# Lane numbers and a triangle of ones kept in PSUM in two edge stages of a graph network kernel; the bias of a third by one product per group

## Chip, cores and metric

The kernel runs on one core of a Trainium2 chip. The metric is its device time in microseconds. The time of the kernel before is 13060.72 us, the median of three runs (13050.09 to 13107.98).

## What is computed

Four graph layers run over 6250 nodes with 128 channels and 206,250 directed edges (100,000 pairs in both directions and 6250 loops), sorted by receiving node `dst`. Each layer normalises `x`, applies relu, and adds its result to `x`. Cut to the parts that the change touches:

```python
# layer 1: runs over src; ew = 0 where src == dst
aggr_out = segment_sum(ew[:, None] * h[dst], src, num_nodes)
deg      = segment_sum(ew, src, num_nodes)
# layer 2: radial weights of an edge from its length, then messages
h = silu(emb @ mlp_w0 + mlp_b0)
h = silu(h @ mlp_w1 + mlp_b1)
w = (h @ mlp_w2 + mlp_b2).reshape(-1, 4, 32)
msg = segment_sum(messages(w, x[src], edge_vec), dst, num_nodes)
# layer 3: a convolution with degrees
agg = segment_sum(h[src] * norm[:, None], dst, num_nodes)
```

## The kernel before

Every layer is a node stage (dense, over all nodes) and an edge stage. An edge stage walks over tiles of 128 edges. Four tiles (U = 4) make a group, and 403 groups (EDGE_GROUPS) make a stage; buffers come in rings of R = 4 groups, and each engine's loop body holds four groups. Each engine runs its own stream of instructions, and semaphores set the order between them. There is no planner: the order of the work is written out by hand. The edge stages are called first to fourth here; the code numbers them 0 to 3.

Because the edges are sorted by `dst`, a tile's receivers lie in a window of 128 nodes that begins at the tile's first `dst` (D0, read into registers by `windows`). A sum over receivers is a product of the gathered rows with a one-hot matrix. The one-hots compare a row of lane numbers 0 to 127 with each edge's number relative to the window (REL). The row of lane numbers, `lane`, and the triangle `K[:, CT:CP]`, which is 1 where the column is smaller than the partition, are columns of the constant tile K in SBUF. `one_hots` (L179 to L184) makes the one-hots of a group in one VectorE tensor_tensor.

**Second edge stage (L833 to L1022).** It sums over `src`, which isn't sorted, so it adds into tables in DRAM by indirect DMA. Per group, VectorE makes `same` (L923: which edges of a tile share a source), four `hotW` (L925: one-hots times weight), `hotB` and `hotA` (L929, L931: low and high part of the receiver's number, for the degrees of the fourth layer), and `before` (L935: `same` times the triangle). The maximum of `before` tells which edge of a source is the last of its tile (L936 to L939), and with it VectorE writes the index of each edge's target row (L942). In every fourth group it also clips the edge lengths (L915, L916) and multiplies the radial basis (L919). TensorE makes psX (L992), psD (L995) and psV (L1001); ScalarE copies psX to `mix` (L975) and psV to `sumrows` (L979). GpSimd (POOL) then issues four scatters with addition, one for each tile (L1015), each to a table of its own. A scatter waits until the one of the same tile of the group before has landed. VectorE's index and ScalarE's `sumrows` are double buffered: they wait until the scatters of two groups back have landed (L940 and L977).

**Third edge stage (L1075 to L1278).** SyncE loads the group's source numbers and its radial basis (L1125, L1126), POOL gathers four tiles of rows (L1139), and VectorE makes the one-hots (L1208, through `one_hots`), the messages `mid` (L1214 to L1230) and adds the window sums (L1200). TensorE's step for group n waits for `hot` and `mid` of n and then interleaves two things: the radial net of group n + 2 (`radial`, L1246) and the window sums of group n (`sums`, L1260). In order: the first layer of the net (L1249), the sums of tiles 0 and 1 (four matmuls, eight instructions, since each fp32 product is two), the second layer (L1252) when ScalarE has made h1 (L1154), the sums of tiles 2 and 3, and the radial weights into psW when ScalarE has made h2 (L1156). For each of the four tiles that is an fp32 product of h2 with w2 (L1256) and a bf16 product that adds the bias (L1257): `three` has ones in three rows, and `b2row` holds the bias cut into three bf16 parts in these rows.

**Fourth edge stage (L1361 to L1427).** SyncE loads source numbers (L1377) when VectorE has finished a group four back. POOL gathers (L1389), TensorE multiplies rows with one-hots (L1425), and VectorE makes the one-hots of the next group (L1409) and then adds four windows (L1412).

Of the kernel before, what the change touches and what calls it, by code (L numbers as in the profile page):

```python
# [6 lines left out]
ALU = mybir.AluOpType  # L7
# [3 lines left out]
P = 128  # L11
# [6 lines left out]
TN = (N + P - 1) // P  # L18
NPAD = (TN + 1) * P
TG = 7  # L20
U = 4
# [89 lines left out]
def build(nc, a, out):  # L111
# [19 lines left out]
    with ctx:  # L131
# [44 lines left out]
        def nodes(table, width):  # L176
            return table[0:TN * P, :].rearrange("(t p) c -> p t c", p=P)[:, :, 0:width]

        def one_hots(dst, n):  # L179

            return nc.vector.tensor_tensor(  # L181
                dst, lane.unsqueeze(1).to_broadcast([P, dst.shape[1], P]),
                REL[:, bass.ds(n * dst.shape[1], dst.shape[1])].unsqueeze(2).to_broadcast([P, dst.shape[1], P]),
                ALU.is_equal)  # L184

# [646 lines left out]
        with ExitStack() as st:  # L832
# [20 lines left out]
            psX = ps("psX1", [P, 2, U, P])  # L853
            psV = ps("psV1", [P, 2, U, 2 * P])
            psD = ps("psD1", [P, 512])
            radius = sb("radius1", [RB, 2 * P])
            cutoff = sb("cutoff1", [RB, 2 * P])
            rounds = EDGE_GROUPS // R
# [7 lines left out]
            with nc.Block() as block:  # L866
# [31 lines left out]
                @block.vector  # L898
                def _(dve):
                    link = Chain(dve, s_chain)  # L900
                    nc.vector.memset(psD[:, 0:TN], 0.0)
                    dve.wait_ge(s_in, 32)
                    link(nc.vector.tensor_scalar(part_i[:, :], dst_i[:, :], P - 1, None, ALU.bitwise_and))
                    link(nc.vector.tensor_copy(low_f[:, :], part_i[:, :]))
                    link(nc.vector.tensor_scalar(part_i[:, :], dst_i[:, :], 7, None, ALU.logical_shift_right))
                    link(nc.vector.tensor_copy(high_f[:, :], part_i[:, :]))
                    link(nc.vector.tensor_copy(other[:, :], dst_i[:, :]))
                    link(nc.vector.tensor_tensor(other[:, :], SRC[:, :], other[:, :], ALU.not_equal))
                    link(nc.vector.tensor_tensor(weight[:, :], weight[:, :], other[:, :], ALU.mult))

                    def step(n, g, r):
                        s = r % 2
                        if r == 0:
                            dve.wait_ge(s_len, 128 * g + 128)
                            nc.vector.tensor_scalar(cutoff[:, :], radius[:, :], 1.0, float(NB ** 0.5), ALU.is_le, ALU.mult)  # L915
                            nc.vector.tensor_scalar(radius[:, :], radius[:, :], 0.0, 1.0, ALU.max, ALU.min).then_inc(s_clip, 1)  # L916
                        if r == 2:
                            dve.wait_ge(s_exp, g + 1)
                            nc.vector.tensor_tensor(radius[:, :], radius[:, :], cutoff[:, :], ALU.mult).then_inc(s_basis, 1)  # L919
                        dve.wait_ge(s_srow[r], 16 * g + 16)  # L920
                        wait_over(dve, s_mix, n - 1)
                        tile_src = SRC[:, bass.ds(n * U, U)]
                        nc.vector.tensor_tensor(same[:, s, :, :], srow[:, r, :, :], tile_src.unsqueeze(2).to_broadcast([P, U, P]), ALU.is_equal).then_inc(s_same, 1)  # L923
                        for u in range(U):
                            last = nc.vector.tensor_scalar(hotW[:, s, u, :], lane, REL[:, bass.ds(n * U + u, 1)],  # L925
                                                           weight[:, bass.ds(n * U + u, 1)], ALU.is_equal, ALU.mult)
                        last.then_inc(s_hot, 1)
                        at = bass.ds(n * U, U)
                        nc.vector.tensor_tensor(hotB[:, s, :, :], lane.unsqueeze(1).to_broadcast([P, U, P]),  # L929
                                                low_f[:, at].unsqueeze(2).to_broadcast([P, U, P]), ALU.is_equal)  # L930
                        nc.vector.tensor_tensor(hotA[:, s, :, :], lane[:, 0:TN].unsqueeze(1).to_broadcast([P, U, TN]),  # L931
                                                high_f[:, at].unsqueeze(2).to_broadcast([P, U, TN]), ALU.is_equal).then_inc(s_node, 1)
                        dve.wait_ge(s_same, n + 1)

                        link(nc.vector.tensor_tensor(before[:, :, :], same[:, s, :, :], K[:, CT:CP].unsqueeze(1).to_broadcast([P, U, P]), ALU.mult))  # L935
                        link(nc.vector.reduce_max(later[:, :], before[:, :, :], axis=AX))  # L936
                        link(nc.vector.tensor_scalar(place[:, :], tile_src, -1.0, K[:, CP:CP + 1], ALU.mult, ALU.add))
                        link(nc.vector.tensor_tensor(place[:, :], place[:, :], later[:, :], ALU.mult))
                        link(nc.vector.tensor_tensor(place[:, :], place[:, :], tile_src, ALU.add))  # L939
                        for u in range(U):  # L940
                            wait_over(dve, s_added[u], 16 * n - 16)
                        nc.vector.tensor_copy(index[:, s, :], place[:, :]).then_inc(s_index, 1)  # L942
                        dve.wait_ge(s_index, n + 1)

                    links = 5
                    link.loop(0, R * links)
                    for r in range(R):
                        step(r, 0, r)
                    link.end(1)
                    with dve.Fori(1, EDGE_GROUPS // R) as g:  # L950
                        link.loop(g - 1, R * links)
                        for r in range(R):
                            step(R * g + r, g, r)
                    link.end(EDGE_GROUPS // R - 1)
                    for n in range(EDGE_GROUPS // R * R, EDGE_GROUPS):
                        step(n, n // R, n % R)
                    dve.wait_ge(s_mix, EDGE_GROUPS)
                    nc.vector.tensor_scalar(DINV[:, :], psD[:, 0:TN], 1.0, None, ALU.add).then_inc(s_root, 1)
                    dve.wait_ge(s_root, 2)
                    link(nc.vector.reciprocal(DINV[:, :], DINV[:, :]))  # L960
# [114 lines left out]
        with ExitStack() as st:  # L1075
# [33 lines left out]
            with nc.Block() as block:  # L1109
# [135 lines left out]
                def _(pe):  # L1245
                    def radial(n, g, r, between=(lambda: None, lambda: None)):  # L1246

                        pe.wait_ge(s_base[r], 16 * g + 16)
                        nc.tensor.matmul(psA[:, 0, :], w0[:, :], base[:, r, :], start=True, stop=True).then_inc(s_h0, 1)  # L1249
                        between[0]()  # L1250
                        pe.wait_ge(s_h1, n + 1)
                        nc.tensor.matmul(psA[:, 1, :], w1[:, :], h1[:, :], start=True, stop=True).then_inc(s_h1p, 1)  # L1252
                        between[1]()
                        pe.wait_ge(s_h2, n + 1)
                        for u in range(U):
                            nc.tensor.matmul(psW[:, r % 2, u, :], h2[:, r % 2, (u % 2) * P:(u % 2 + 1) * P], w2[:, u // 2, :], start=True, stop=False)  # L1256
                            done = nc.tensor.matmul(psW[:, r % 2, u, :], three[:, :], b2row[:, :], start=False, stop=True)  # L1257
                        done.then_inc(s_w, 1)

                    def sums(n, r, tiles):  # L1260
# [100 lines left out]
        with ExitStack() as st:  # L1361
# [4 lines left out]
            rows = sb("rows3", [P, R, U, C])  # L1366
            hot = sb("hot3", [P, 2, U, P])
            psS = ps("psS3", [P, 4, 512])
            s_chain, s_hot, s_sum, s_free, s_done = (sem(n + "_e3") for n in ("s_chain", "s_hot", "s_sum", "s_free", "s_done"))
            s_rows = gathered3  # L1370
            s_index = sem("s_index_e3", R)
            with nc.Block() as block:
# [24 lines left out]
                @block.vector  # L1397
                def _(dve):
                    link = Chain(dve, s_chain)
                    link(nc.vector.memset(ACC[:, 0, :], 0.0))  # L1400
                    dve.sem_inc(s_done, R)
                    dve.sem_inc(s_free, 4)
                    one_hots(hot[:, 0, :, :], 0).then_inc(s_hot, 1)

                    def add(n, g, r):
                        if not (isinstance(n, int) and n == last):
                            one_hots(hot[:, (r + 1) % 2, :, :], n + 1).then_inc(s_hot, 1)
                        firsts = windows(dve, n * U)
                        for u in range(U):  # L1409
                            dve.wait_ge(s_sum, n * U + (u + 1))  # L1410
                            own = ACC[:, 0, bass.ds(firsts[u], P)]
                            nc.vector.tensor_tensor(own, own, psS[:, u, 0:P], ALU.add).then_inc(s_free, 1)  # L1412
                            dve.wait_ge(s_free, n * U + (u + 5))
                        dve.sem_inc(s_done, 1)
# [128 lines left out]
```

## Time and profile before

| | |
|---|---|
| median of three runs | 13060.72 us |
| the profiled execution | 13058.8 us |
| its span, first to last instruction | 13057.0 us |
| POOL busy | 7574.9 us (58%) |
| VectorE (DVE) busy | 6520.0 us (50%) |
| TensorE (PE) busy | 6219.0 us (48%) |
| mean granted TensorE clock | 0.585 |

The profile shows one execution. Times in it are microseconds from the span's start, unless marked ns. PE is TensorE's matmul and PEld its weight load, DVE is VectorE, ACT ScalarE, POOL GpSimd, SP SyncE. L12 is line 12 of the kernel. `out<-in` names the tiles that an instruction writes and reads. The granted clock is a share of 2.4 GHz. A releaser is what ended an engine's idle time by the semaphores' events; "issue" means that the profile shows nothing that the engine waited for. Lengths in the POOL rows are those of issuing an indirect DMA, not of its transfer.

### The profile page before, as it was taken

To read this page: it belongs to the slowest core of one execution; us is meant where nothing else is said; L and a number is where in the kernel's file an instruction comes from. 1 tells how busy PE (TensorE), PEld (TensorE's weight loads), DVE (VectorE), ACT (ScalarE), POOL (GpSimd) and SP (SyncE) were. 2 spreads that over 40 slices of the span, in tenths; PEclk is the share of its full clock that TensorE was granted. 3 is DMA by queue.
4 is the path that set the end of the run, shared out by engine and by line. 5 is a ranking of instruction groups with operands and counts; after the bars stand their busy time and mean duration, and the time that the engine had idled before them with its cause. 6 is when DMAs were issued, how large, how long until landed. Compare 5 with 4: busy or idle time off the path is not lost. (4 is left out here: it accounts for less than half of the span.)

```text
span 13057.0 us, 156203 instructions
## 1 busy us (share of the span) xinstructions
PE 6219.0 (48%) x30616; PEld 5225.2 (40%) x30616; DVE 6520.0 (50%) x17016; ACT 1617.6 (12%) x2488; POOL 7574.9 (58%) x6452
## 2 busy tenths in 40 slices
PE   1333333333335555555554477777777533333332
PEld 1222222222234444444443366666666423333332
DVE  3444444444445556555555566666666522232224
ACT  0111111111111111111111011111111100000000
POOL 2544445444228888888886255555555266666663
PEclk7555555555555555555555687787888755555555
DMA  3323223223536666666666111111111111111111
GB/s 89 75 75 75 74 75 75 75 75 75 92 52 96 102 98 104 100 103 100 100 99 118 36 40 38 38 39 39 40 39 40 28 43 43 43 43 44 43 42 46
DMA packets 1206936, 865.00 MB, mean 66 GB/s; under 512 B 523976, under 2 KB 1040463, under 8 KB 1206294
## 3 DMA queue, kind: packets, MB, share of 16 engines
q0 software_dynamic: 386880, 430.42, 19.4%
q1 hardware_dynamic: 818812, 430.82, 14.1%
q10 hardware_dynamic: 1036, 1.96, 0.1%
q14 instruction: 195, 1.60, 0.0%
q8 instruction: 13, 0.21, 0.0%
HBM read 712.60 MB, written 149.81 MB: 66 GB/s over the span
## 5 line engine op out<-in xcount | busy, mean ns | idle before, releaser
L1015 POOL DMA_INDIRECT sums<-sumrows,index x1612 | 2809.7, 1743 | 858.4 <-ACT sumrows L979 385.1
L529 POOL DMA_INDIRECT rows<-table,index x1612 | 1621.7, 1006 | 1833.1 <-DMA index<-in_src_batches 1351.8
L1139 POOL DMA_INDIRECT rows<-table,index x1612 | 1573.9, 976 | 1557.6 <-DMA index<-in_src_groups 1028.6
L1389 POOL DMA_INDIRECT rows<-table,index x1612 | 1569.4, 974 | 1100.4 <-DMA index<-in_src_groups 622.6
L1425 PE MATMUL psS<-hot,rows 128*128 128x128 f32 x3224 | 957.0, 463 | 1549.1 <-DMA rows<-table,index 564.3
L1425 PEld LDWEIGHTS psS<-hot,rows 128*128 128x128 f32 x3224 | 769.1, 319 | 1737.0 <-issue 927.1
L992 PE MATMUL psX<-same,hotW 128*128 128x128 f32 x3224 | 833.3, 440 | 1273.8 <-DVE hotW L925 1076.6
L992 PEld LDWEIGHTS psX<-same,hotW 128*128 128x128 f32 x3224 | 715.8, 327 | 1391.4 <-DVE hotW L925 1180.5
L667 DVE TENSOR_TENSOR ACC<-ACC,psA 128x128 f32 x1612 | 462.5, 287 | 1603.6 <-remote 754.5
L1412 DVE TENSOR_TENSOR ACC<-ACC,psS 128x128 f32 x1612 | 465.8, 289 | 1391.4 <-issue 838.9
L1264 PEld LDWEIGHTS psS<-hot,mid 128*128 128x128 f32 x6448 | 1020.3, 233 | 206.1 <-issue 143.2
L1264 PE MATMUL psS<-hot,mid 128*128 128x128 f32 x6448 | 1098.8, 325 | 2.3 <-DVE mid L1230 2.3
L1200 DVE TENSOR_TENSOR ACC<-ACC,psS 128x256 f32 x1612 | 672.2, 417 | 769.0 <-PE psS L1264 416.0
L1001 PE MATMUL psV<-win,mix 128*128 128x129 f32 x3224 | 819.9, 433 | 346.6 <-ACT mix L975 308.3
L1001 PEld LDWEIGHTS psV<-win,mix 128*128 128x128 f32 x3224 | 703.4, 321 | 398.2 <-issue 398.2
L1256 PE MATMUL psW<-w,h 128*128 128x128 f32 x3224 | 684.4, 339 | 245.5 <-issue 131.1
L181 DVE TENSOR_TENSOR hot<-K,REL 128x512 f32<-128x512 f32 x806 | 556.0, 690 | 378.1 <-issue 198.4
L1256 PEld LDWEIGHTS psW<-w,h 128*128 128x128 f32 x3224 | 580.0, 225 | 304.9 <-issue 144.7
L942 DVE CAST index<-place 128x4 int32<-128x4 f32 x403 | 82.8, 206 | 1186.7 <-DMA sums<-sumrows,index 1179.2
L735 PE MATMUL psA<-HN,rows 128*128 128x128 f32 x1624 | 458.9, 442 | 122.6 <-DVE ACC L667 111.0
L735 PE MATMUL psA<-ACC,rows 128*128 128x128 f32 x1600 | 454.4, 444 | 105.8 <-DVE ACC L667 95.4
L1252 PE MATMUL psA<-h,w 128*128 128x256 f32 x806 | 333.6, 504 | 317.5 <-issue 178.2
(266 smaller groups left out, 9601.4 us busy)
## 6 DMA issues: line engine op xcount, KB each, us to landing
win<-table SPq DMA_DIRECT2D x1612, 64.5 KB
srow<-src_f SPq DMA_DIRECT2D x403, 256.0 KB
rows<-table,index POOLq DMA_INDIRECT x4836
HN<-rel_f SPq DMA_DIRECT2D x102, 512.0 KB
relB<-rel_f SPq DMA_DIRECT2D x102, 512.0 KB
er<-limbs SPq DMA_DIRECT2D x1632, 3.0 KB
sums<-sumrows,index POOLq DMA_INDIRECT x1612
ACC<-edge_marks SPq DMA_DIRECT2D x204, 96.0 KB
```

The source lines that it names most:

```text
L181: return nc.vector.tensor_tensor(dst, lane.unsqueeze(1).to_broadcast([P, dst.shape[1], P]), REL[:, bass.ds(n * dst.shape[1], dst.shape[1]) ...
L529: nc.gpsimd.indirect_dma_start(out=rows[:, r, k, :], out_offset=None, in_=table0[:, :], in_offset=bass.IndirectOffsetOnAxis(ap=index[:, r, ...
L735: nc.tensor.matmul(psA[:, k % 4, 0:P], rows[:, r, k, 0:C], hots[s][:, k, :], start=True, stop=True).then_inc(s_sum, 1)
L992: last = nc.tensor.matmul(psX[:, s, u, :], hotW[:, s, u, :], same[:, s, u, :], start=True, stop=True)
L1001: last = nc.tensor.matmul(psV[:, s, u, 0:W1], mix[:, s, u, :], win[:, r, u, :], start=True, stop=True)
L1015: nc.gpsimd.indirect_dma_start(out=sums1[u][:, :], in_=sums[:, s, u, :], in_offset=None, compute_op=ALU.add, out_offset=bass.IndirectOffse ...
L1139: nc.gpsimd.indirect_dma_start(out=rows[:, r, u, :], out_offset=None, in_=table2[:, :], in_offset=bass.IndirectOffsetOnAxis(ap=index[:, r, ...
L1200: nc.vector.tensor_tensor(own, own, psS[:, u, :, 0:P], ALU.add).then_inc(s_free, 1)
L1256: nc.tensor.matmul(psW[:, r % 2, u, :], h2[:, r % 2, (u % 2) * P:(u % 2 + 1) * P], w2[:, u // 2, :], start=True, stop=False)
L1264: done = nc.tensor.matmul(psS[:, u, b, 0:P], mid[:, r % 2, u, b * C:(b + 1) * C], hot[:, r % 2, u, :], start=True, stop=True)
L1389: nc.gpsimd.indirect_dma_start(out=rows[:, r, u, :], out_offset=None, in_=table3[:, :], in_offset=bass.IndirectOffsetOnAxis(ap=index[:, r, ...
L1425: nc.tensor.matmul(psS[:, u, 0:P], rows[:, r, u, :], hot[:, r % 2, u, :], start=True, stop=True).then_inc(s_sum, 1)
```

## The change

In the second edge stage a new PSUM tile psK1 takes a copy of the lane numbers (`numbers`) and of the triangle (`below`), written once by VectorE ahead of the loop. hotB, hotA and `before` read these in place of `lane` and `K[:, CT:CP]`; hotW keeps `lane`. In the fourth edge stage a PSUM tile psK3 takes the lane numbers, and `one_hots` reads them there through its new argument. `one_hots` in the first and third stages keeps `lane`. In the third stage the four bias products of a group become one, over all four tiles' columns of psW, with `b2row` repeated four times as the moving operand. It is issued behind the first layer's product and starts the accumulation; the fp32 products then add to it.

```diff
--- before.py
+++ after.py
@@ -176,10 +176,10 @@
         def nodes(table, width):
             return table[0:TN * P, :].rearrange("(t p) c -> p t c", p=P)[:, :, 0:width]
 
-        def one_hots(dst, n):
+        def one_hots(dst, n, numbers=lane):
 
             return nc.vector.tensor_tensor(
-                dst, lane.unsqueeze(1).to_broadcast([P, dst.shape[1], P]),
+                dst, numbers.unsqueeze(1).to_broadcast([P, dst.shape[1], P]),
                 REL[:, bass.ds(n * dst.shape[1], dst.shape[1])].unsqueeze(2).to_broadcast([P, dst.shape[1], P]),
                 ALU.is_equal)
 
@@ -853,6 +853,8 @@
             psX = ps("psX1", [P, 2, U, P])
             psV = ps("psV1", [P, 2, U, 2 * P])
             psD = ps("psD1", [P, 512])
+            psK = ps("psK1", [P, 4, P])
+            numbers, below = psK[:, 0, :], psK[:, 1, :]
             radius = sb("radius1", [RB, 2 * P])
             cutoff = sb("cutoff1", [RB, 2 * P])
             rounds = EDGE_GROUPS // R
@@ -899,6 +901,8 @@
                 def _(dve):
                     link = Chain(dve, s_chain)
                     nc.vector.memset(psD[:, 0:TN], 0.0)
+                    nc.vector.tensor_copy(numbers, lane)
+                    link(nc.vector.tensor_copy(below, K[:, CT:CP]))
                     dve.wait_ge(s_in, 32)
                     link(nc.vector.tensor_scalar(part_i[:, :], dst_i[:, :], P - 1, None, ALU.bitwise_and))
                     link(nc.vector.tensor_copy(low_f[:, :], part_i[:, :]))
@@ -926,13 +930,13 @@
                                                            weight[:, bass.ds(n * U + u, 1)], ALU.is_equal, ALU.mult)
                         last.then_inc(s_hot, 1)
                         at = bass.ds(n * U, U)
-                        nc.vector.tensor_tensor(hotB[:, s, :, :], lane.unsqueeze(1).to_broadcast([P, U, P]),
+                        nc.vector.tensor_tensor(hotB[:, s, :, :], numbers.unsqueeze(1).to_broadcast([P, U, P]),
                                                 low_f[:, at].unsqueeze(2).to_broadcast([P, U, P]), ALU.is_equal)
-                        nc.vector.tensor_tensor(hotA[:, s, :, :], lane[:, 0:TN].unsqueeze(1).to_broadcast([P, U, TN]),
+                        nc.vector.tensor_tensor(hotA[:, s, :, :], numbers[:, 0:TN].unsqueeze(1).to_broadcast([P, U, TN]),
                                                 high_f[:, at].unsqueeze(2).to_broadcast([P, U, TN]), ALU.is_equal).then_inc(s_node, 1)
                         dve.wait_ge(s_same, n + 1)
 
-                        link(nc.vector.tensor_tensor(before[:, :, :], same[:, s, :, :], K[:, CT:CP].unsqueeze(1).to_broadcast([P, U, P]), ALU.mult))
+                        link(nc.vector.tensor_tensor(before[:, :, :], same[:, s, :, :], below.unsqueeze(1).to_broadcast([P, U, P]), ALU.mult))
                         link(nc.vector.reduce_max(later[:, :], before[:, :, :], axis=AX))
                         link(nc.vector.tensor_scalar(place[:, :], tile_src, -1.0, K[:, CP:CP + 1], ALU.mult, ALU.add))
                         link(nc.vector.tensor_tensor(place[:, :], place[:, :], later[:, :], ALU.mult))
@@ -1247,14 +1251,14 @@
 
                         pe.wait_ge(s_base[r], 16 * g + 16)
                         nc.tensor.matmul(psA[:, 0, :], w0[:, :], base[:, r, :], start=True, stop=True).then_inc(s_h0, 1)
+                        nc.tensor.matmul(psW[:, r % 2, :, :], three[:, :], b2row[:, :].unsqueeze(1).to_broadcast([P, U, P]), start=True, stop=False)
                         between[0]()
                         pe.wait_ge(s_h1, n + 1)
                         nc.tensor.matmul(psA[:, 1, :], w1[:, :], h1[:, :], start=True, stop=True).then_inc(s_h1p, 1)
                         between[1]()
                         pe.wait_ge(s_h2, n + 1)
                         for u in range(U):
-                            nc.tensor.matmul(psW[:, r % 2, u, :], h2[:, r % 2, (u % 2) * P:(u % 2 + 1) * P], w2[:, u // 2, :], start=True, stop=False)
-                            done = nc.tensor.matmul(psW[:, r % 2, u, :], three[:, :], b2row[:, :], start=False, stop=True)
+                            done = nc.tensor.matmul(psW[:, r % 2, u, :], h2[:, r % 2, (u % 2) * P:(u % 2 + 1) * P], w2[:, u // 2, :], start=False, stop=u == U - 1)
                         done.then_inc(s_w, 1)
 
                     def sums(n, r, tiles):
@@ -1366,6 +1370,7 @@
             rows = sb("rows3", [P, R, U, C])
             hot = sb("hot3", [P, 2, U, P])
             psS = ps("psS3", [P, 4, 512])
+            numbers = ps("psK3", [P, 512])[:, 0:P]
             s_chain, s_hot, s_sum, s_free, s_done = (sem(n + "_e3") for n in ("s_chain", "s_hot", "s_sum", "s_free", "s_done"))
             s_rows = gathered3
             s_index = sem("s_index_e3", R)
@@ -1397,14 +1402,15 @@
                 @block.vector
                 def _(dve):
                     link = Chain(dve, s_chain)
+                    nc.vector.tensor_copy(numbers, lane)
                     link(nc.vector.memset(ACC[:, 0, :], 0.0))
                     dve.sem_inc(s_done, R)
                     dve.sem_inc(s_free, 4)
-                    one_hots(hot[:, 0, :, :], 0).then_inc(s_hot, 1)
+                    one_hots(hot[:, 0, :, :], 0, numbers).then_inc(s_hot, 1)
 
                     def add(n, g, r):
                         if not (isinstance(n, int) and n == last):
-                            one_hots(hot[:, (r + 1) % 2, :, :], n + 1).then_inc(s_hot, 1)
+                            one_hots(hot[:, (r + 1) % 2, :, :], n + 1, numbers).then_inc(s_hot, 1)
                         firsts = windows(dve, n * U)
                         for u in range(U):
                             dve.wait_ge(s_sum, n * U + (u + 1))
```

## Rows read from the trace of the kernel before

**Rows 1.** Windows: the second, third and fourth edge stage, with column names.

```profile
core 0: us, PE busy (x) PEld busy (x) DVE busy (x) ACT busy (x) POOL busy (x), PEclk, DMA share, GB/s
3820.00:7125.00 3305.00, 1713.45 (x8036) 1519.68 (x8034) 1952.30 (x5522) 565.53 (x1006) 2809.74 (x1612) 0.51 0.66 100
7366.00:10275.00 2909.00, 2264.86 (x12896) 1880.89 (x12896) 1847.44 (x5238) 508.73 (x905) 1573.88 (x1612) 0.81 0.16 39
10448.00:12933.00 2485.00, 956.99 (x3224) 769.12 (x3224) 737.48 (x2011) 0.00 (x0) 1569.44 (x1612) 0.50 0.17 43
```

**Rows 2.** Groups by line, second stage: busy us, mean ns, idle before it, releasers.

```profile
L1015 POOL DMA_INDIRECT sums<-sumrows,index x1612 | 2809.7, 1743 | 858.4 <-ACT sumrows L979 385.1 <-issue 349.9 <-DMA sums<-sumrows,index 121.2
...
L942 DVE CAST index<-place 128x4 int32<-128x4 f32 x402 | 82.7, 206 | 1186.6 <-DMA sums<-sumrows,index 1179.2 <-issue 3.9 <-DVE place L939 3.3
```

**Rows 3.** Line L1015 by itself: minimum, median and maximum in ns.

```profile
L1015 POOL DMA_INDIRECT sums<-sumrows,index x1612: 1541/1542/3251, 3820.5 to 7121.8; - x180
```

**Rows 4.** Timeline, second stage: start, length, line, [idle before it, releaser].

```profile
3820.52 1.61 POOL L1015 DMA_INDIRECT sums<-sumrows,index  x1 [365.29 <-ACT sumrows L979]
...
5003.68 0.68 DVE L935 TENSOR_TENSOR before<-same,K 128x512 f32<-128x512 f32 x1
5003.87 1.90 POOL L1015 DMA_INDIRECT sums<-sumrows,index  x1 [0.30 <-issue]
...
5015.31 3.20 POOL L1015 DMA_INDIRECT sums<-sumrows,index  x1 [0.30 <-DMA sums<-sumrows,index]
5015.54 0.68 DVE L929 TENSOR_TENSOR hotB<-K,low_f 128x512 bf16<-128x512 f32 x1
...
5016.42 0.68 DVE L935 TENSOR_TENSOR before<-same,K 128x512 f32<-128x512 f32 x1
...
7103.62 3.13 POOL L1015 DMA_INDIRECT sums<-sumrows,index  x1 [0.30 <-DMA sums<-sumrows,index]
```

**Rows 5.** Timeline, fourth stage, VectorE and POOL.

```profile
11501.28 0.69 DVE L181 TENSOR_TENSOR hot<-K,REL 128x512 f32<-128x512 f32 x1 [2.54 <-issue]
...
11512.28 0.69 DVE L181 TENSOR_TENSOR hot<-K,REL 128x512 f32<-128x512 f32 x1 [0.26 <-DVE ACC L1412]
...
11515.67 0.29 DVE L1412 TENSOR_TENSOR ACC<-ACC,psS 128x128 f32 x1
11515.80 0.94 POOL L1389 DMA_INDIRECT rows<-table,index  x1 [0.30 <-issue]
...
11518.15 0.69 DVE L181 TENSOR_TENSOR hot<-K,REL 128x512 f32<-128x512 f32 x1 [0.67 <-DVE ACC L1412]
11518.30 1.35 POOL L1389 DMA_INDIRECT rows<-table,index  x1 [0.30 <-issue]
```

**Rows 6.** Groups by line, fourth stage (first row) and third stage.

```profile
L1389 POOL DMA_INDIRECT rows<-table,index x1612 | 1569.4, 974 | 1100.4 <-DMA index<-in_src_groups 622.6 <-issue 477.7
...
L1200 DVE TENSOR_TENSOR ACC<-ACC,psS 128x256 f32 x1612 | 672.2, 417 | 769.0 <-PE psS L1264 416.0 <-DMA K<-in_consts 322.1 <-issue 25.2
...
L1214 DVE TENSOR_TENSOR dot<-rows,HN 128x384 f32<-128x384 f32 x403 | 222.6, 552 | 10.8 <-DMA rows<-table,index 8.2 <-issue 2.6
...
L1226 DVE TENSOR_TENSOR mid<-psW,rows 128x384 f32<-128x384 f32 x403 | 221.8, 550 | 0.0
...
L1252 PE MATMUL psA<-h,w 128*128 128x256 f32 x806 | 333.6, 504 | 317.5 <-issue 178.2 <-ACT h L1154 139.0
L1249 PE MATMUL psA<-base,w 16*128 16x256 f32 x806 | 329.0, 492 | 138.2 <-DMA base<-basis 61.6 <-DVE mid L1230 51.1 <-issue 17.1
```

**Rows 7.** Windows: the stretch of the third stage shown next.

```profile
9011.00:9021.00 10.00, 8.14 (x60) 6.66 (x58) 7.14 (x20) 1.42 (x3) 6.89 (x7) 1.00 0.19 50
```

**Rows 8.** Timeline, TensorE, third stage, granted clock 1.00.

```profile
9011.56 0.22 PE L1257 MATMUL psW<-b2row,three 128*128 128x128 bf16 x1
9011.61 0.44 PE L1256 MATMUL psW<-w,h 128*128 128x128 f32 x2
9011.89 0.22 PE L1257 MATMUL psW<-b2row,three 128*128 128x128 bf16 x1
...
9015.36 1.05 PE L1264 MATMUL psS<-hot,mid 128*128 128x128 f32 x8
```

## What I expect and why

> **What bounds the kernel now.** I read the page first for the span and its slices, then the stage windows, because the three edited loops stand in separate stages with separate limits. The second edge stage takes 3305 us, the third 2909, the fourth 2485 [rows 1]: 8699 of 13057 us. The rest is not touched.
>
> *Second stage.* GpSimd (POOL) is busy 2809.7 us with its 1612 scatters, mean 1743 ns [rows 2], and its timeline shows about 0.30 us between one scatter and the next, over and over [rows 4]. 1612 x (1.743 + 0.305) = 3301 us, which is the stage. So POOL sets the end here: VectorE waits 1179.2 us for scatters to land before it may write the next index [rows 2], and is busy 1952 us of 3305 [rows 1]. The scatter's median is 1542 ns, its minimum 1541, its maximum 3251 [rows 3]. The distance between mean and median is what can be won: 1612 x (1743 - 1542) = 324 us.
>
> Who lengthens them? A scatter that starts at 5015.31 takes 3.20 us. VectorE runs hotW, hotB, hotA and `before` meanwhile, without a gap, the last from 5016.42 to 5017.10. The one that starts at 5003.87 takes 1.90, and `before` ends at 5004.36 [rows 4]. 5017.10 + 1.41 = 5018.51 is the end of the first, 5004.36 + 1.41 = 5005.77 that of the second. Both ended 1.41 us after `before` did: they stood still near their start until VectorE's chain was over. Taken so over all 1612, 447 are lengthened by over 30 ns, 323 us together, the first at 3820.52 and the last at 7103.62 [rows 4]; 287 us belong to scatters let go at the end of `before`. All 77 that start during hotB are lengthened. One that starts during hotW is let go after about 0.1 us if another hotW follows, but mostly not where the last hotW passes into hotB.
>
> *The operand decides.* In the fourth stage the gather that starts at 11515.80, beside the add of a PSUM tile (L1412), takes the normal 0.94 us. The one at 11518.30, beside the one-hots of L181, whose two inputs lie in SBUF, takes 1.35: L181 ends at 11518.84, and 0.81 later, at 11519.65, the gather ends [rows 5]. Every lengthened gather of that stage, 184 of 1612, was let go by L181, none by L1412.
>
> **The change, part by part.**
>
> *Second stage.* Three VectorE operations of each step get a PSUM operand: hotB, hotA and `before`, 0.68, 0.35 and 0.68 us long. Their own time: a 128x384 form with one PSUM input takes 550 ns (L1226), with two SBUF inputs 552 (L1214) [rows 6]; I take nothing, with both ends at nothing. The two copies ahead of the loop cost under 1 us. What goes is the standing still at these three. What stays is `same` (L923, two SBUF inputs), the four hotW, and L915 to L919 of every fourth step. Today about 36 us of lengthening are let go by these, the lower bound of what stays. For the upper bound, since scatters will start at other places of VectorE's chain, one step in three has a scatter that waits out a whole `same` and L919 ahead of it: 403/3 x 1.0 = 134 us. I take 55, nearer to what is seen. Saved: 324 - 55 = 269 us, bounds 190 and 288.
>
> What is late next? Without lengthening a step is 4 x (1.542 + 0.305) = 7.39 us of POOL. VectorE is busy 1952/403 = 4.8 us a step, TensorE 1713/403 = 4.3 [rows 1]: both have over 2 us left. The index and the sums were there before POOL came for them: apart from the first wait of 365.29 us POOL's gaps are its 0.30 [rows 2, 4].
>
> *Fourth stage.* L181 gets a PSUM operand. The gathers' mean is 974 ns [rows 6], the median 944: 1612 x 0.030 = 48 us of lengthening. POOL needs 4 x (0.974 + 0.30) = 5.10 us a step, 2055 us in all; the stage takes 2485. It waits 622.6 us for index loads [rows 6], and these wait for VectorE, which has stretches where one step takes 11.0 us (11501.28 to 11512.28) [rows 5] and it stands idle with nothing that the profile names. The 48 us are won while POOL leads and lost while VectorE lags. Bounds 0 and 48; I take 40, since few one-hots fall into the slow stretches.
>
> *Third stage.* Out go four bf16 products (L1257), each behind a pair of fp32 products (L1256). In comes one of 512 columns, behind the first product of the radial net (L1249) and ahead of the sums (L1264). At a granted clock of 1.00, 2.4 GHz [rows 7], the groups of a pair and a bias follow each other every 0.33 us (9011.56, 9011.89). A pair alone is 0.22: the eight products of half a step's sums take 1.05 us, less 0.28 for the length of the last, so 0.77/7 = 0.11 from one to the next [rows 8]. So the tail of a step gets shorter by 4 x 0.11 = 0.44 us. The new product costs four times the distance from a bias product to its successor (9011.56 to 9011.61, some 0.055 us): 0.22 us. At 1.2 GHz I take both double, 0.88 and 0.44. The stage's clock is 0.81 [rows 1], so 62% of it runs at full rate. Tail: 403 x (0.62 x 0.44 + 0.38 x 0.88) = 245 us off. Front: 122 us on.
>
> Which of the two is on the path? TensorE waits only 51.1 us for `mid` at the start of a step [rows 6], so mostly the tail of one step sets the start of the next; there the net of both counts, 122 us. But VectorE waits 769.0 us ahead of its adds (L1200) [rows 6]; queued behind the new product are all eight sums of the first half, and the adds wait for them. And where TensorE waits for ScalarE (L1252, 317.5 us [rows 6]) the front product may hide in that wait. Bounds: 245 us won (only the tail counts) and 122 lost (only the front counts). I take 50 won, under half of the net, since POOL's pace of about 5.1 us a step hides it where nothing is late. The stage's mean is 2909/403 = 7.2.
>
> **The sum.** 269 + 40 + 50 = 359 us. The profiled execution took 13058.8 us, 1.8 over its span and 2 below the median of the three runs, 13060.72. 13058.8 - 359 = 12,700.
>
> **A rule that speaks against this.** In the second stage all 77 scatters that started beside hotB stood still, and hotB is a tensor_tensor with two SBUF inputs [rows 4]. The Trainium skill ("SBUF — State Buffer", section "Who interferes with whom") infers that such an operation does not hold up descriptor generation, since it takes only the read side of the port pair that VectorE shares with GpSimd. By that rule the moves to PSUM would give nothing. The same section says that two SBUF inputs contend with a GpSimd instruction that reads SBUF; these DMAs take their index from SBUF, and the trace agrees with that sentence.
>
> **The rivals.**
> 1. *The standing still moves.* With a steady 7.39 us step POOL's starts may lock onto `same` or L919 instead, and one scatter a step waits 0.5 us: 403 x 0.5 = 202 us stay. 324 - 202 = 122 saved, with 90 from the other stages: 12,847. For it: `same` follows a landing by a fixed time. Against: the starts around it cost little today.
> 2. *The third stage loses.* Fewer weight loads let the clock fall to 0.50 for good, or the front product counts in full. With 0.5 us more for each step of 7.2, 200 us: 13058.8 - 269 - 40 + 200 = 12,950. Against: the bias columns of a step are the same 512.
> 3. *The operand doesn't matter, or the change doesn't do what it says.* Something else in hotB and `before` holds POOL. Then only the third stage's 50 us are left: 13,009. Against: the pair of gathers in [rows 5].
> 4. *Slower.* In the fourth stage the slow stretches spread, because POOL runs freer and VectorE catches up and waits more often. A slow step costs 11.0 - 5.1 = 5.9 us over POOL's pace; today's are (2485 - 2055)/5.9 = some 73. From 359/5.9 = 61 more the whole gain is gone; at 85 more the time is 12,700 + 85 x 5.9 = 13,200. For it: the slow stretches are not explained. Against: they end where POOL waits.
> 5. *More than that.* The tail counts in full and the slow steps of the fourth stage get fewer by 9 (50 us): 13058.8 - 288 - 245 - 48 - 50 = 12,428.
>
> **How the numbers follow.** Forecast 0.70 (own range 12,580 to 12,830), rival 1 0.12, rival 2 0.06, rivals 3, 4 and 5 0.04 each. The range reaches from the forecast's lower bounds, with two thirds of the tail (13058.8 - 288 - 48 - 163 = 12,560), to rival 1 and a little over it, 12,870. A measurement of this kernel tells about 0.5% (65 us) from no change. Faster by over that: forecast, rivals 1, 2 and 5, 0.92. Within: rival 3, 0.04. Slower: rival 4, 0.04.
>
> **What the profile after would show.** Second stage: scatters with a mean of 1.56 to 1.60 us and none over 2.5, their gaps still 0.30, the stage about 3035 us, hotB, hotA and `before` as long as now; a scatter that starts beside hotB takes 1.54. Fourth stage: gathers with a mean of 0.944, POOL's wait for indices about as now. Third: pairs of psW products every 0.22 us at full clock, one bias product a step, the clock near 0.81. I am wrong if scatters beside hotB are still lengthened, if VectorE's forms with PSUM take longer than now, or if POOL's gaps open because index or sums come late.

## The result, and the profile after

The changed kernel takes 12,774.27 us, the median of four runs (12,744.97 to 12,782.68); the kernel before, run beside it, 13,083.67. The ratio is 0.976, with an interval of 0.973 to 0.979. The forecast was 12,700 with a range of 12,560 to 12,870. The profiled execution took 12,782.7 us, 276 less than that of before; the forecast was 359 less. By the medians it is 309 less: the profiled execution is the slowest of the four of the changed kernel.

The windows of the three edited stages, changed kernel (columns as in [rows 1]):

```profile
3816.00:6830.00 3014.00, 1721.94 (x8034) 1526.57 (x8032) 1973.03 (x5521) 566.56 (x1006) 2520.67 (x1612) 0.51 0.71 109
7070.00:9947.00 2877.00, 2117.55 (x11687) 1770.81 (x11687) 1831.39 (x5240) 509.42 (x905) 1584.09 (x1612) 0.81 0.16 39
10122.00:12647.00 2525.00, 991.64 (x3204) 778.72 (x3204) 730.32 (x1997) 0.00 (x0) 1522.22 (x1612) 0.50 0.17 42
```

From POOL's first indirect DMA of a stage to the end of its last, by the trace:

| stage | before | after | difference | forecast |
|---|---|---|---|---|
| second | 3302.9 us | 3012.8 us | -290.1 us | -269 us |
| third | 2888.1 us | 2855.8 us | -32.3 us | -50 us |
| fourth | 2476.1 us | 2524.6 us | +48.5 us | -40 us |

So the second stage gave a little more than forecast, the third a little less, and the fourth went the other way. POOL's rows of the page (mean ns behind the busy time, then the idle time and what ended it):

```profile
L1019 POOL DMA_INDIRECT sums<-sumrows,index x1612 | 2520.7, 1564 | 854.2 <-ACT sumrows L983 394.5
...
L1394 POOL DMA_INDIRECT rows<-table,index x1612 | 1522.2, 944 | 1198.2 <-DMA index<-in_src_groups 685.6
```

The scatter's mean fell from 1743 to 1564 ns [rows 2], with the same idle time between scatters. The gather of the fourth stage fell from 974 to 944 ns [rows 6], as forecast, but POOL's wait for index loads there rose from 622.6 to 685.6 us. What the scatters meet now can be read in the timeline of the second stage, changed kernel:

```profile
5009.61 0.68 DVE L933 TENSOR_TENSOR hotB<-psK,low_f 128x512 bf16<-128x512 f32 x1
5009.79 1.54 POOL L1019 DMA_INDIRECT sums<-sumrows,index  x1 [0.30 <-issue]
...
5015.33 1.59 POOL L1019 DMA_INDIRECT sums<-sumrows,index  x1 [0.30 <-issue]
5015.55 0.67 DVE L933 TENSOR_TENSOR hotB<-psK,low_f 128x512 bf16<-128x512 f32 x1
...
5016.42 0.67 DVE L939 TENSOR_TENSOR before<-same,psK 128x512 f32<-128x512 f32 x1
```

The scatter at 5015.33 stands in the same place as the one of 3.20 us in [rows 4], in the last hotW and ahead of hotB, and takes 1.59. One that starts beside hotB takes 1.54. VectorE's operations are as long as they were (groups by line, second stage, changed kernel):

```profile
L933 DVE TENSOR_TENSOR hotB<-psK,low_f 128x512 bf16<-128x512 f32 x401 | 271.7, 677 | 0.0
L939 DVE TENSOR_TENSOR before<-same,psK 128x512 f32<-128x512 f32 x401 | 269.5, 672 | 0.0
```

### The profile page after: what moved, and what is told of

Same layout as the page of the kernel before. It is cut to its first block and busy times, and to the rows that moved or that the text cites. A ratio compares the mean times of both kernels' runs of the same rounds, so it can differ in the third digit from the quotient of the medians.

```text
span 12780.9 us, 153789 instructions
## 1 busy us (share of the span) xinstructions
PE 6128.6 (48%) x29407; PEld 5141.5 (40%) x29407; DVE 6521.6 (51%) x17019; ACT 1619.1 (13%) x2488; POOL 7245.6 (57%) x6452
## 5 line engine op out<-in xcount | busy, mean ns | idle before, releaser
L1019 POOL DMA_INDIRECT sums<-sumrows,index x1612 | 2520.7, 1564 | 854.2 <-ACT sumrows L983 394.5
L1394 POOL DMA_INDIRECT rows<-table,index x1612 | 1522.2, 944 | 1198.2 <-DMA index<-in_src_groups 685.6
L1431 PE MATMUL psS<-hot,rows 128*128 128x128 f32 x3224 | 997.3, 472 | 1559.2 <-DVE ACC L1418 671.1
L1268 PEld LDWEIGHTS psS<-hot,mid 128*128 128x128 f32 x6448 | 1050.8, 231 | 58.6 <-issue 3.0
L1268 PE MATMUL psS<-hot,mid 128*128 128x128 f32 x6448 | 1038.6, 315 | 2.7 <-DVE mid L1234 2.3
L1261 PE MATMUL psW<-w,h 128*128 128x128 f32 x3224 | 524.5, 315 | 363.2 <-ACT h L1160 190.0
L1261 PEld LDWEIGHTS psW<-w,h 128*128 128x128 f32 x3224 | 475.4, 226 | 389.5 <-ACT h L1160 203.8
L181 DVE TENSOR_TENSOR hot<-psK,REL 128x512 f32<-128x512 f32 x403 | 278.6, 691 | 426.0 <-issue 235.1
L929 DVE TENSOR_SCALAR hotW<-K,REL,weight 128x128 f32<-128x128 f32 x1612 | 455.7, 365 | 0.0
```

The source lines that it names most:

```text
L1019: nc.gpsimd.indirect_dma_start(out=sums1[u][:, :], in_=sums[:, s, u, :], in_offset=None, compute_op=ALU.add, out_offset=bass.IndirectOffse ...
L1261: done = nc.tensor.matmul(psW[:, r % 2, u, :], h2[:, r % 2, (u % 2) * P:(u % 2 + 1) * P], w2[:, u // 2, :], start=False, stop=u == U - 1)
L1268: done = nc.tensor.matmul(psS[:, u, b, 0:P], mid[:, r % 2, u, b * C:(b + 1) * C], hot[:, r % 2, u, :], start=True, stop=True)
L1394: nc.gpsimd.indirect_dma_start(out=rows[:, r, u, :], out_offset=None, in_=table3[:, :], in_offset=bass.IndirectOffsetOnAxis(ap=index[:, r, ...
L1431: nc.tensor.matmul(psS[:, u, 0:P], rows[:, r, u, :], hot[:, r % 2, u, :], start=True, stop=True).then_inc(s_sum, 1)
```

## The experiments

The experiments ran on three chips on which the kernel before takes 10,763 to 10,777 us, not 13,084: in the first, third and fourth stages no engine answers late there. To answer late means here that an engine takes us longer than usual for its next step and the profile names nothing that it waits for; the last section has the numbers. Each experiment is compared with runs of before on its own chip. Stage lengths are again from POOL's first indirect DMA to the end of its last.

### The second stage alone, and where the operand lies

`s2_only` makes only the second stage's part of the change.

> Only the second stage's part is made: hotB, hotA and `before` read the lane numbers and the triangle from PSUM. Theory (POOL's scatters stand still beside VectorE operations with two SBUF inputs): the stage goes from 3303 us of POOL's first to last scatter to about 3013, as in the changed kernel, mean scatter 1.56 us; third and fourth stage as before; ratio 0.978. Rival (the parts help one another, or the gain is the third stage's): a gain of under 200 us, ratio over 0.985.

Measured: 10,450.17 us, ratio 0.970 (0.967 to 0.973). The stage takes 3012.9 us, scatters 1563 ns; the others are as before. The ratio is lower than the 0.978 expected: the stage unchanged takes 3302 to 3349 us in the seven profiles on these chips that have it so, against 3303 in the first pair, and the whole is shorter.

`s2_copy_in_sbuf` has the same instructions, with the copy in SBUF:

```diff
-            psK = ps("psK1", [P, 4, P])
+            psK = sb("copyK1", [P, 4, P])
```

> The same instructions as in the second stage's part, but the copy of the lane numbers and of the triangle lies in SBUF, not in PSUM. Theory (the operand's place decides): the scatter's mean stays at 1.74 us, the stage at 3303, ratio 1.00. Rival (a tile apart from the constants, or the position of the code, decides): mean near 1.56, ratio 0.978.

Measured: 10,763.58 us, ratio 0.999 (0.997 to 1.001). POOL's row in the page of each, `s2_only` first, then `s2_copy_in_sbuf`:

```profile
L1019 POOL DMA_INDIRECT sums<-sumrows,index x1612 | 2520.2, 1563 | 842.9 <-ACT sumrows L983 382.9 <-issue 331.2 <-DMA sums<-sumrows,index 122.4
```

```profile
L1019 POOL DMA_INDIRECT sums<-sumrows,index x1612 | 2851.1, 1769 | 844.7 <-ACT sumrows L983 366.0 <-issue 349.8 <-DMA sums<-sumrows,index 127.7
```

The place of the copy, PSUM or SBUF, is the whole difference between the two sources: 206 ns for each of 1612 scatters, 331 us. The rival that something else in these operations holds POOL falls, and so does the one that a tile apart from the constants is enough.

`s2_only_before` moves the triangle alone:

```diff
-     nc.vector.tensor_tensor(before[...], same[...], K[:, CT:CP]..., ALU.mult)
+     nc.vector.tensor_tensor(before[...], same[...], below..., ALU.mult)
```

> Second stage: only `before` reads the triangle from PSUM, hotB and hotA keep the lane numbers in SBUF. Theory (a scatter stands still until the chain of operations with two SBUF inputs ends): it is now let go at the end of hotA, 0.66 us earlier; 237 scatters x 0.66 = 156 us won, ratio near 0.985, largest lengthening about 1.0 us in place of 1.7. Rival (`before` alone holds the scatters): as the whole part, 320 us, ratio 0.970.

Measured: 10,603.96 us, ratio 0.986 (0.983 to 0.989), 159 us against the 156 expected; the stage 3170.4 us, mean scatter 1662 ns. Its timeline shows the chain cut short by one link:

```profile
4016.39 2.55 POOL L1019 DMA_INDIRECT sums<-sumrows,index  x1 [0.30 <-ACT sumrows L983]
4016.56 0.68 DVE L933 TENSOR_TENSOR hotB<-K,low_f 128x512 bf16<-128x512 f32 x1
4017.16 0.35 DVE L935 TENSOR_TENSOR hotA<-K,high_f 128x196 bf16<-128x196 f32 x1
4017.43 0.67 DVE L939 TENSOR_TENSOR before<-same,psK 128x512 f32<-128x512 f32 x1
```

hotA ends at 4017.51; 1.41 us later is 4018.92, and the scatter ends at 4018.94. It is let go by the last operation with two SBUF inputs, not by `before`. It is not alone: 302 lengthened scatters of this run end 1.35 to 1.46 us after a hotA, and they hold 172 of its 192 us of lengthening. In the kernel before, 237 end so after a `before`, with 287 of 323 us.

### The fourth and the third stage alone, and all of the change

> Only the fourth stage's part: the one-hots read the lane numbers from PSUM. In the changed kernel no gather of this stage is lengthened, yet the stage took 2525 us in place of 2476. Theory A (freer gathers bring more of VectorE's slow stretches): 2525 us again, ratio 1.004. Theory B (the slow stretches vary from run to run, and the profile of the changed kernel had more of them): the stage between 2430 and 2530, the ratio 0.996 to 1.000. Lengthening 0 in both.

Measured: 10,703.31 us, ratio 0.994 (0.991 to 0.996). No gather is lengthened, and the stage takes 2012.3 us; in the other kernels of that chip with this stage unchanged it takes 2060.0 to 2061.5. So 48 us of lengthening give 48 us of the stage. By the medians the kernel is 71 us faster; the interval of the ratio reaches from 44 to 95 us, so the times agree with 48 but don't show it by themselves. The ratio lies below what either theory named, since both were worked out for a stage with slow stretches, and here there were none. This run can't tell A from B, therefore.

> Only the third stage's part: one bias product of 512 columns at the front of a step. Theory (the tail counts with the front against it): third stage 2888 us goes to about 2850, ratio 0.997; fourth stage as before, 2476. Rival (all of the shorter tail is won, or the front costs as much): 2640, ratio 0.98, or 2888 and more, ratio 1.000 or over.

Measured: 10,760.20 us, ratio 1.000 (0.998 to 1.001): nothing. The window of the third stage of `s3_only`:

```profile
6349.00:8384.00 2035.00, 1666.41 (x11657) 1421.97 (x11658) 1850.05 (x5222) 509.43 (x905) 1543.13 (x1612) 1.00 0.23 56
```

1612 x (0.957 + 0.305) = 2034 us is POOL's pace, and it is the stage. Whatever TensorE saves lies under it. Theory and rival were both worked out for a stage of 2888 us, which this chip did not have; the 0.997 of the theory lies outside the interval.

> The whole change once more, beside the single parts of the first set. There the fourth and third stages ran at POOL's pace without late answers of any engine (2061 and 2034 us, no idle of POOL over its 0.3 us). If the parts add up there: 320 us of the second stage, 48 of the fourth, 0 of the third, ratio 0.966, near 10,406 us. If the slow stretches of the fourth stage come back with the change alone, that stage is over 2100 us and the ratio near 0.975.

Measured: 10,406.76 us, ratio 0.967 (0.964 to 0.970). The expectation was 10,406. The parts add up: second stage 3014.5 us, third 2035.5, fourth 2015.1. The fourth stage does not get its slow stretches from the change alone.

### The third stage with POOL's bound taken off

To see the bias product at all, the next kernels gather only two of four tiles in the third stage. The other two tiles' rows are set to zero once and their messages are left out, so these kernels serve for timing only:

```diff
-                        for u in range(U):
+                        for u in range(U // 2):
                             nc.gpsimd.indirect_dma_start(
                                 out=rows[:, r, u, :], ..., in_=table2[:, :],
```

> The kernel before with POOL's bound taken off the third stage: it gathers two of the four tiles of a group, and the rows of the other two are zeros (their messages are left out). For comparison with the next. POOL then needs 2.5 us a step, so VectorE (4.6 us) or TensorE sets the pace: stage near 403 x 4.7 = 1900 us if VectorE, over 2000 if TensorE at half clock counts.

> As the one before, with the third stage's part of the change (one bias product at the front); the same two tiles are left out. It measures what the bias product is worth where POOL doesn't hide it. Theory of the prediction (net of tail and front on the path): 0.22 to 0.44 us a step where TensorE sets the pace, at most 120 us less than the one before. Rival (the front delays the sums, the adds and so the next step): up to 120 us more. If VectorE alone sets the pace: equal within 20 us.

Measured: 10,547.68 us without the change of the bias, 10,593.35 with it: 46 us slower. The stage takes 1802.3 and 1863.5 us, so it costs 61 us there; in the two profiles the second stage, the same in both, differs by 18 us the other way (3335.1 and 3317.5). Window and two groups of each, first `s3_half_gather`, then `s3_half_gather_change`:

```profile
6357.00:8160.00 1803.00, 1762.22 (x12809) 1501.27 (x12808) 1769.59 (x5198) 507.47 (x902) 781.32 (x806) 0.99 0.14 33
...
L1201 DVE TENSOR_TENSOR ACC<-ACC,psS 128x256 f32 x1596 | 659.1, 413 | 18.8 <-PE psS L1265 3.7
...
L1250 PE MATMUL psA<-base,w 16*128 16x256 f32 x804 | 279.6, 427 | 101.3 <-DMA base<-basis 62.8 <-DVE mid L1231 2.1
```

```profile
6342.00:8207.00 1865.00, 1658.88 (x11603) 1415.21 (x11604) 1775.46 (x5197) 507.42 (x902) 779.68 (x806) 1.00 0.14 32
...
L1201 DVE TENSOR_TENSOR ACC<-ACC,psS 128x256 f32 x1596 | 658.7, 413 | 75.9 <-PE psS L1265 47.0
...
L1250 PE MATMUL psA<-base,w 16*128 16x256 f32 x804 | 280.1, 427 | 267.8 <-DVE mid L1231 204.9 <-DMA base<-basis 62.9
```

VectorE sets the pace, with 1770 of 1803 us busy. The change does shorten TensorE's work, by 103 us of busy time, but TensorE only waits for `mid` longer with it (2.1 to 204.9 us). The product at the front makes the sums late, and VectorE stands 57 us longer ahead of its adds (18.8 to 75.9 us). The expectation for this case, equal within 20 us if VectorE alone sets the pace, missed this: VectorE's adds stand behind the sums, and the sums behind the new product.

The two prices in the prediction's sum can be read where the clock is full. From the first psW product of a step to the end of the last takes 1.44 us with four bias products (median of `s3_half_gather`) and 1.06 without them (`s3_half_gather_change`), so the tail gets 0.38 us shorter, for 0.44 taken. At the front, from the timeline of `full_again`:

```profile
7000.89 0.39 PE L1254 MATMUL psW<-b2row,three 128*128 128x512 bf16 x1
...
7001.12 1.05 PE L1268 MATMUL psS<-hot,mid 128*128 128x128 f32 x8
...
7003.33 1.06 PE L1261 MATMUL psW<-w,h 128*128 128x128 f32 x8
```

The sums start 0.23 us after the new product, for 0.22 taken. Both sides of the sum exist, and in the half-gather kernels only the front counts.

Is it the place, or the product of 512 columns as such? Two kernels tell, run on one chip: the product behind the second half of the sums, just ahead of the wait for h2, and the half-gather kernel once more beside it.

```diff
                         nc.tensor.matmul(psA[:, 0, :], w0[:, :], base[:, r, :], ...).then_inc(s_h0, 1)
-                        nc.tensor.matmul(psW[:, r % 2, :, :], three[:, :], b2row[...]..., start=True, stop=False)
                         between[0]()
...
                         between[1]()
+                        nc.tensor.matmul(psW[:, r % 2, :, :], three[:, :], b2row[...]..., start=True, stop=False)
                         pe.wait_ge(s_h2, n + 1)
```

> As s3_half_gather_change, with the one bias product behind the second half of the sums, ahead of the wait for h2; the messages of two of four tiles are left out here too. At the front it cost 46 us (10,593 against 10,548). If it is the place in front of the sums that costs (0.22 us a step ahead of the adds), the loss is gone: 10,548 or some us less. If the one product of 512 columns itself costs, as against four of 128: still near 10,590.

> s3_half_gather once more, on the same chip as the one above, so that the two can be compared with each other; messages of two of four tiles are left out. 10,548 us if the chip is like the last one.

Measured: 10,549.74 us late, 10,554.83 for the half-gather kernel, so the loss is gone in the times. The stage takes 1812.7 us late, against 1802.4, so 10 us of the 61 are left in the profiles; VectorE's idle time ahead of the adds is 23.6 us, not 75.9. It is the place in front of the sums that costs.

> The kernel before with only the third stage's bias product, in the late place. Where POOL sets that stage's pace (no late answers): 0 within 10 us, ratio 1.000. On a chip where engines answer late as in the first profile: 50 to 120 us less in that stage, since the shorter tail counts and nothing stands ahead of the sums; ratio 0.992 to 0.996.

Measured: 10,758.92 us, ratio 0.999 (0.998 to 1.000); the stage 2034.0 us, POOL's pace again. What it is worth with late answers was not seen: no chip of the experiments showed them.

### A version meant to beat both

`all_four_late` has the whole change, the bias product in the late place, and the lane numbers in PSUM in the first and third stages as well:

```diff
             psP = ps("psAlpha0", [P, 512])
+            numbers = psP[:, 2 * P:3 * P]
...
-                            done = one_hots(hots[s][...], 4 * n + q)
+                            done = one_hots(hots[s][...], 4 * n + q, numbers)
```

> A version meant to beat both: the whole change, and the lane numbers in PSUM in the first and the third stage too (in the first in columns of psAlpha0 that nothing else uses), and the bias product of the third stage behind the second half of the sums, just ahead of the wait for h2, instead of at the front. Where no engine answers late, the first stage is at POOL's pace (2219 us, 128 of it lengthening, 122 of that during its one-hots): theory 120 us less there, 1 in the third, near 10,286 us, ratio 0.956. Rival (the first stage waits for something else once its gathers are freer): 10,380 to 10,406, ratio 0.965.

Measured: 10,389.99 us, ratio 0.964 (0.962 to 0.966), beside 0.967 for the whole change on another chip: the rival's case. POOL's row of the first stage, `full_again` first, then `all_four_late`:

```profile
L529 POOL DMA_INDIRECT rows<-table,index x1612 | 1653.2, 1026 | 776.5 <-issue 486.0 <-DMA index<-in_src_batches 290.5
```

```profile
L530 POOL DMA_INDIRECT rows<-table,index x1612 | 1530.8, 950 | 881.5 <-issue 476.8 <-DMA index<-in_src_batches 404.7
```

The gathers get 122 us shorter, as expected (8 of 128 us of lengthening are left), and POOL waits 114 us more for its index loads. The stage goes from 2219.6 to 2203.6 us. VectorE gives these loads free, once its batch is done, and 1430 of 2204 us busy is no bound by itself; which of its waits comes last there was not taken apart. The two intervals overlap, so a gain over the changed kernel is not shown by the times.

## Why the prediction was right, and where not

- **What bounds the second stage: right.** POOL sets it and nothing else was near. The 324 us between the scatter's mean and its median were the right measure of what could be won: 290 of them were won in the first pair. 32 us of lengthening are left over 150 scatters, against the 55 that I took; the lower bound, 36 us of today's, was the better value. Rival 1, that POOL's starts lock onto `same`, did not come.
- **Why scatters stand still: right, and shown.** The operand's place decides (`s2_only` against `s2_copy_in_sbuf`), and the end of the chain of two-SBUF-input operations lets the scatter go (`s2_only_before`). The sentence of the Trainium skill ("SBUF — State Buffer", "Who interferes with whom") that infers that a tensor_tensor does not hold up descriptor generation does not hold for these indirect DMAs: 1769 ns with the second input in SBUF, 1563 with it in PSUM. The same section of the Trainium skill also says that two SBUF inputs contend with a GpSimd instruction that reads SBUF, and that fits. Whether it is the reading of the index that stands still was not shown; no kernel had the index elsewhere.
- **VectorE's own time with a PSUM input: right.** 677 and 672 ns for hotB and `before`, against 679 and 680.
- **The fourth stage: right in the mechanism, wrong in the sum of the first pair.** The 48 us of lengthening went to nothing. Without late answers they are won in full (`s4_only`). In the first pair the stage got 48.5 us longer, outside the bounds of 0 to 48 won: the step that failed is that a stage with slow stretches keeps as many of them. In the trace the steps of VectorE of over 8 us took 1488 us together before and 1626 after. The trace also shows where the time went: register, branch and semaphore instructions of VectorE of over 0.5 us number 945 in this stage before, 674 us together, and 1091 after, 784 us; in the twelve profiles of the experiments there are none. This is the direction of rival 4, but whether the freer gathers bring it about or it varies from run to run stays open, since no experiment met such stretches. One profile of each kernel can't settle it: the four times of the kernel before differ among themselves by 58 us, those of the changed kernel by 38. The adds of this stage after:

```profile
L1418 DVE TENSOR_TENSOR ACC<-ACC,psS 128x128 f32 x1598 | 460.9, 288 | 1369.0 <-issue 915.8 <-remote 168.8 <-PE psS L1431 147.9
```

  Most of the idle time ahead of them ends with "issue", nothing that the profile names. In `s4_only` the same adds wait 950.5 of 1126.0 us for TensorE's sums, which wait for gathers.
- **The third stage: the value was a guess that one pair can't confirm.** 32 us went in the first pair, for 50 forecast, and nothing shows that the bias product won them. TensorE's waits of over 2 us ahead of the second layer's product, where it needs ScalarE's h1, came to 196 us before (58 waits) and 139 after (29); there are none in `full_again` or `s3_only`. That is 57 us less, more than the 32 us by itself, and whether it varies from run to run or comes with the change was not tested. The prices of the tail and of the front were near (0.38 us for 0.44, 0.23 for 0.22); which of them is on the path was the guess. Where POOL sets the pace it is nothing, and where VectorE does, the front costs 61 us of the stage, 46 of the time. My reason for a gain, that TensorE seldom waits for `mid` [rows 6], can hold only while late answers keep TensorE behind, and no experiment met those. The half-gather kernels show what decides: who waits for what is queued behind the new product.
- **The sum.** 269 + 50 + 40 = 359 us forecast, 290 + 32 - 48 = 274 found in the profiles. The miss is nearly the 88 us of the fourth stage; the third stage's 18 too few and the second's 21 too many cancel, which is luck. The time still lies in the range because the second stage, the part with the firm reason, is most of the sum.
- **The clock** stayed at 0.81 in the third stage: rival 2 did not come.

## What to carry to other kernels

When POOL issues indirect DMAs back to back and sets the pace, compare the mean of their issue time with its median and look which VectorE operation ends a fixed time (here 1.41 us for a scatter, 0.81 for a gather) before the long ones do. Here a constant operand of that operation moved to PSUM cost one copy and freed POOL, but only the lengthening of a stage that runs at POOL's pace turns into time. An instruction merged and moved to the front of a step is paid by all that is queued behind it; the same one behind the work that others wait for was free here.

## What the runs showed of the hardware

- The indirect DMA of POOL stands still as long as VectorE runs one operation with two SBUF inputs after another: up to 1.7 us on top of 1.54 in the first profile. Between two hotW operations it mostly gets its turn, but not always: a scatter of `s4_only` took 3.83 us, 2.3 on top, and stood still over three further hotW, hotB, hotA and `before`; `s3_only` and `s3_half_gather_change` have one such each. In the second and fourth stages of the changed kernel none was held for over 0.1 us beside operations with one PSUM input, reductions and copies alone. In the first stage of `all_four_late` the one-hots with PSUM input held one for 0.14 us and other operations, such as the scans, up to 0.19.
- The same program took 13,084 us in the first pair and 10,763 to 10,777 on the three chips of the experiments. The difference lies in three stages. Those with gathers take 3246, 2888 and 2476 us in the first profile and 2219, 2034 and 2061 in the later ones, while the second stage, with scatters, takes 3303 and 3302 to 3349. What is late differs by stage. In the fourth, register instructions of VectorE take 0.7 us in place of 0.04 at times (945 of them over 0.5 us in the first profile), and in the first stage some of VectorE (207) and more of SyncE (789) do. In the third, those of VectorE are all as short as ever; there SyncE has 111 of them, and ScalarE lets TensorE wait up to 8.3 us for h1. The third stage's granted clock is 0.81 there and 1.00 in the later ones, at the same work. What causes it, and whether it goes with the chip, is open.
